# fp16 halves of the normalised input: made in natural layout and turned by DMA transposes

## What is computed

```python
xn = layernorm(x)                                   # (2, 1024, 512)
q, k, v = xn @ Wq.T, xn @ Wk.T, xn @ Wv.T           # 16 heads of 32
attn = softmax(causal(q @ k.T / sqrt(32)))
s = (attn @ v) @ Wo.T
hidden = silu(xn @ W1.T) * (xn @ W3.T)              # (2, 1024, 2048)
g = silu(fwht(hidden) @ W2.T)                       # Walsh-Hadamard transform
out = x + s * g
```

## Time and profile before

| | |
|---|---|
| median of 2 runs | 951.73 us (951.0 to 952.46) |
| span of the profiled execution | 949.5 us |
| PE busy | 936.6 us (99%) |
| VectorE busy | 728.2 us (77%) |
| ScalarE busy | 613.9 us (65%) |
| GpSimd busy | 340.2 us (36%) |

### The profile page before, as it was taken

One profiled execution on the slowest core, in us unless ns is written; L12 is line 12 of the kernel. 1 busy time (PEld: TensorE's weight loads), 2 busy tenths in 40 slices (PEclk: granted clock), 3 DMA queues, 4 the chain that ended last, 5 costly groups with the idle time before them and its releaser, 6 DMA issues. The chain is left out here.

```text
span 949.5 us, 18956 instructions
## 1 busy us (share of the span) xinstructions
PE 936.6 (99%) x6498; PEld 635.5 (67%) x6498; DVE 728.2 (77%) x1407; ACT 613.9 (65%) x1316; POOL 340.2 (36%) x590
## 2 busy tenths in 40 slices
PE   8999999999999999999999999999999999999997
PEld 7765556666665656888888656656666666588886
DVE  7987998998998988746565579899899898833343
ACT  4445889888888886723344358887888878832221
POOL 1896663665665442000000114344453443500000
PEclk9999999999999999999999999999999999999999
DMA  9797346543342405961136623323223231190111
GB/s 290 255 271 217 89 114 157 144 115 101 101 123 69 124 23 179 355 215 59 48 115 229 200 56 81 88 62 102 64 79 91 57 95 42 46 370 29 45 45 45
DMA packets 57920, 118.48 MB, mean 125 GB/s; under 512 B 5600, under 2 KB 22624, under 8 KB 57312
## 3 DMA queue, kind: packets, MB, share of 16 engines
q1 hardware_dynamic: 57824, 117.27, 40.8%
HBM read 83.43 MB, written 33.55 MB: 123 GB/s over the span
## 5 line engine op out<-in xcount | busy, mean ns | idle before, releaser
L1178 DVE TENSOR_TENSOR p_lo<-stages,p_hi 128x512 f16<-128x512 f32 (+2 forms) x288 | 199.7, 703 | 24.9 <-ACT p_hi L844 24.0
L1516 PE MATMUL f<-x_hi,w_lo 128*128 128x512 f16 x512 | 195.6, 382 | 0.0
L1516 PE MATMUL f<-x_lo,w_hi 128*128 128x512 f16 x512 | 194.8, 380 | 0.0
L1516 PE MATMUL f<-x_hi,w_hi 128*128 128x512 f16 x512 | 194.5, 380 | 0.0
L834 ACT ACTIVATE stages<-s 128x512 f32<-128x512 f32 (+2 forms) x288 | 150.5, 523 | 57.9 <-PE s L1476 55.3
L844 ACT ACTIVATE p_hi<-stages 128x512 f16<-128x512 f32 (+2 forms) x288 | 160.3, 557 | 27.5 <-POOL stages L670 18.6
L1476 PE MATMUL s<-qk_st 98*128 98x512 f32 (+2 forms) x384 | 130.0, 417 | 0.4 <-DMA qk_st<-m_lo 0.3
L670 POOL TENSOR_SCALAR_AFFINE_SELECT stages<-stages 128x128 f32<-128x128 f32 x192 | 61.5, 326 | 164.9 <-ACT stages L834 164.5
L678 POOL TENSOR_TENSOR w_lo<-w,w_hi 128x256 f16<-128x256 f32 x128 | 95.5, 775 | 55.2 <-ACT w_hi L876 52.8
L1165 DVE CUSTOM_DVE_ANT_0 m<-m,causal 128x1024 f32<-128x1024 f32 (+1 forms) x98 | 104.5, 1066 | 2.7 <-PE m L1457 1.3
L1245 DVE TENSOR_TENSOR h_lo<-hidden,h_hi 128x1024 fp32r<-128x1024 f32 x32 | 39.2, 1224 | 84.6 <-ACT h_hi L927 84.6
(11 more groups left out here) (208 smaller groups left out, 1989.1 us busy)
## 6 DMA issues: line engine op xcount, KB each, us to landing
qk_st<-qk_parts SPq DMA_DIRECT2D x96, 256.0 KB, 4.4
w<-w1w SPq DMA_DIRECT2D x32, 512.0 KB, 3.6
qk_parts<-qk_hi SPq DMA_DIRECT2D x32, 256.0 KB, 3.5
qk_parts<-qk_lo SPq DMA_DIRECT2D x32, 256.0 KB, 4.2
scan<-w1w SPq DMA_DIRECT2D x12, 512.0 KB, 5.3
wht_in<-w SPq DMA_DIRECT2D x4, 1024.0 KB, 10.6
w_butterflied<-wht_in SPq DMA_DIRECT2D x4, 1024.0 KB, 5.7
w_transformed<-g_hi SPq DMA_DIRECT2D x8, 512.0 KB, 3.7
```

The lines of the kernel that those rows point to most:

```text
L1178: dve.tensor_tensor(p_lo[s][:], expd[q % NE][:, 0:end - need], p_hi[s][:], ALU.subtract).then_inc(p_lo_done, 1)
L1516: mm = pe.matmul(F[m][:, 0, :], w, v, start=k == 0, stop=k == GMM - 1)
```

## The change

The fp16 parts are no longer made from the PSUM transposes. ACT makes `xn_hi` (128 rows x 512 columns, fp16) from the tile of `xb`, VectorE `xn_lo` from `xb` and `xn_hi`, at the same places of the order as `x16` before. Then SP issues two DMA transposes, `xn_hi` to `x16_hi` and `xn_lo` to `x16_lo`. There are two slots for each of `xn_hi` and `xn_lo`: the nth tile's ACT operation waits until both DMAs of tile n - 2 have landed. The V groups wait for the landing in place of `x16_lo_done`. SP waits for all of them after group 11, before the stack loads, since the slots share memory with a stack. PE's transposes into a bank wait for `xt_lo` of four tiles earlier only; so do the two matmul steps that use bank M.

```diff
+            with ExitStack() as q:
+                xn_hi = [sb(f"xn_hi{i}", [P, D], F16, q) for i in range(2)]
+                xn_lo = [sb(f"xn_lo{i}", [P, D], F16, q) for i in range(2)]
             qk_st.insert(0, sb("qk_st0", [P, 2, S], F32R, r))
...
+        def x16_slot(b, t):
+
+            return (x16_no(b, t) - 1) % 2
+
+        def x16_landed(no):
+
+            return (no + 1) // 2 * 32
...
+                    for t in X16_AFTER.get(g, ()):
+                        transpose_x16(b, t)
                     if g == FIRST_STACK:
 
+                        for i in range(2):
+                            sp.wait_ge(x16_in[i], x16_landed((b + 1) * NT - 1 + i))
...
+            def transpose_x16(b, t):
+                slot = x16_slot(b, t)
+                sp.wait_ge(xn_lo_done, x16_no(b, t))
+                for dst, src in ((x16_hi, xn_hi), (x16_lo, xn_lo)):
+                    sp.dma_start_transpose(dst[:, :, t * P:(t + 1) * P], src[slot][:]).then_inc(x16_in[slot], 16)
...
             def x16(b, t):
-                act.wait_ge(xt_lo_done, b * NT + t + 1)
-                act.activation(x16_hi[:, :, t * P:(t + 1) * P], xt_bank(t).rearrange("p (k c) -> p k c", k=KT),
-                               ACT.Copy, scale=X_TOP).then_inc(x16_hi_done, 1)
+                no, slot = x16_no(b, t), x16_slot(b, t)
+                act.wait_ge(xn_done, b * NT + t + 1)
+                if b > 0 and no == b * NT + 1:
+                    for i in range(2):
+                        act.wait_ge(y_stored[i], 1 + b * (NT // 2) * 16)
+                if no > 2:
+                    act.wait_ge(x16_in[slot], x16_landed(no - 2))
+                act.activation(xn_hi[slot][:], xb[:, t, :], ACT.Copy, scale=X_TOP).then_inc(xn_hi_done, 1)
...
             def x16(b, t):
-                dve.wait_ge(x16_hi_done, x16_no(b, t))
-                at = (slice(None), slice(None), slice(t * P, (t + 1) * P))
-                dve.scalar_tensor_tensor(x16_lo[at], xt_bank(t).rearrange("p (k c) -> p k c", k=KT), X_TOP,
-                                         x16_hi[at], ALU.mult, ALU.subtract).then_inc(x16_lo_done, 1)
+                slot = x16_slot(b, t)
+                dve.wait_ge(xn_hi_done, x16_no(b, t))
+                dve.scalar_tensor_tensor(xn_lo[slot][:], xb[:, t, :], X_TOP, xn_hi[slot][:], ALU.mult, ALU.subtract
+                                         ).then_inc(xn_lo_done, 1)
...
             def transpose_xn(b, t):
                 pe.wait_ge(xn_done, b * NT + t + 1)
                 if t >= 4:
-                    pe.wait_ge(x16_lo_done, x16_no(b, t - 4))
+                    pe.wait_ge(xt_lo_done, b * NT + t - 3)
...
                         pe.wait_ge(wv_lo_done, (b + 1) * KT)
-                        pe.wait_ge(x16_lo_done, x16_no(b, t))
+                        pe.wait_ge(x16_in[x16_slot(b, t)], x16_landed(x16_no(b, t)))
```

## The result

The changed kernel takes 965.06 us (median of 2 runs, 964.79 to 965.33) against 951.73: a ratio of 1.0133, interval 1.0099 to 1.0167. That is 13.3 us slower. The time lies inside the forecast range, 8 us under the forecast itself, on the faster side of the likeliest case (970 to 990) and inside that of rival 1. A loss over 2% had been given 0.57, one within 2%, which came, 0.42.

A forecast was written before the change was run, and what follows sets the result against it. PE bounds the kernel, busy 936.6 of 949.5 us. To 951.7 the prediction added 19.2 for batch 0 (VectorE's waits and contention) and 2.5 for batch 1: 973.4, forecast 973 us, range 958 to 1012 for 8 in 10.

The forecast's parts named there:

- the likeliest case: Transposing DMAs on SP's queue with an issue of 1.2 to 2.2 us: 970 to 990 us, chance 0.41.
- rival 1: At ACT's slot wait: DMAs as quick as plain ones, loss too small to tell; 956 to 970 us, chance 0.38.
- the first chain: Batch 0: ACT waits for slots, VectorE for ACT; group 8 starts 9.5 us later, the V groups 19.2.
- pair 6: Batch 0: the sixth tile's two DMAs land at 63.2 and cost VectorE 0.7 us of waiting.
- the wait before the transposes of `v_scale`: PE in the changed profile, batch 0: idle some 5 us there.
- The freed bank: PSUM bank free earlier: PE's 0.5 us wait goes, but only brings PE sooner to group 8.
- L: Time from VectorE's release of a DMA pair to its landing: 2 x 1.5 + 4.5 = 7.5 us.
- the contention: VectorE's low part slowed beside POOL, about 1.48 us each: +7.0 us in batch 0, 0 in batch 1.
- the forecast case: The likeliest case: transposing issues of 1.2 to 2.2 us on SP's queue, 970 to 990 us, chance 0.41.
- the stack loads are hidden by 2 us or more: SP at group 11, ahead of the first `qk_st` loads: waiting for landings costs nothing, with 2 us or more to spare.
- rival 2: DMAs hold SP's queue 3 us each or more: 1004 us at 3.0 and 4.5, 1029 at 4 and 6; chance 0.17.
- +2.5: Batch 1, group 8: `xt_lo` 7 ends at 514.8 instead of 511.3, less 1.0 us of slack.

The follow-up runs named there:

- four_slots: The changed kernel with four slots instead of two for xn_hi and xn_lo: 965.2 us, ratio 1.0134.
- unwaited: The kernel before, with sixteen transposing DMAs per batch added on SP's queue into memory that nothing reads: 966.04 us, ratio 1.0139.
- after: The changed kernel itself, against the kernel before: 965.06 us, ratio 1.0133.
- four_slots_scan: The changed kernel with four slots and the scan load issued after group 6 instead of 10: 962.85 us, ratio 1.0117.

## Why the prediction was right, and where it was wrong

**Right: the sign, and the first chain.** ACT waits for slots at the tiles named (third, fourth, and the one after group 8) and VectorE idles there; PE is late at group 8 and the V groups. The waits forecast as 4.9, 2.4 and 6.1 us were 2.31, 0.99 and 3.87. The fourth, 0.7 for pair 6, wasn't there; 0.41 stands in its stretch, before a `qk_lo`, because ACT's copy came late. PE waited 4.71 and 2.77 us, where near 10, 5 and 5 had been forecast; the wait before the transposes of `v_scale` did not come. The freed bank brought no gain that can be seen.

**Mis-sized: L.** It was put at 7.5 us, 2 x 1.5 of issue and 4.5 to the landing. Measured for the first pair: released at 26.43 + 0.69 = 27.12, landed at 32.46, so L = 5.3, of which 2.6 are the issues. The term that was off is the landing behind the last issue, 2.7 instead of 4.5; it had been taken from stores of 256 KB in a crowded stretch. By the Trainium skill ("Advanced Engine Details and Errata", X-Bar Transpose (TRN2)) transposing DMAs are as fast as regular ones: for the landing the runs agree (medians from the start of the issue, 2.9 and 3.2 us), for the hold on the queue they don't (1.26 and 0.63 us).

**Mis-sized: the contention.** The low part took 8.68 us for eight in batch 0. By the prediction's own way that is 8.68 - 8 x 0.60 = +3.9, not +7.0. The first ran before POOL began; of the seven beside POOL's steps two took 0.7 all the same and five 1.1 to 1.8, and what sets which is not shown. `wv_lo`, the nearest row, took 1490 ns again.

With both sizes put right the same chain gives VectorE +6.0 of idle time (2.31 + 0.99 + 3.87 + 0.41 and 0.68 more before a `qk_lo`, less the 2.24 of before), +3.9, and about -1 of other steps (`wv_abs` and `v_scale` shorter by 1.6, the scaling of Wv longer by 0.5): +8.9, against +19.2 forecast; group 8 +3.5 instead of +9.5. It is rival 1's case (L under 6.9), though the issues were not as quick as that rival wanted; it held 0.38 of the chance where the forecast case held 0.41.

**Wrong: that the stack loads are hidden by 2 us or more.** The step looked only at the batch in which everything else is late. The whole content of SP's queue moves with its sixteen issues, and four_slots and unwaited show that this alone costs what the change costs. The prediction carried it only as part of L and in rival 2, at 3 us each.

**Right size by luck, wrong place: batch 1.** +2.5 was forecast at group 8 through `xt_lo` 7. Group 8 lost nothing (+10.65 behind the kernel before, as the first scores of batch 0 were +10.2). The 2.5 us come at the first use of a stack, and SP's queue in order of time says why:

```profile
537.95 1.23 SPq L520 DMA_TRANSPOSE x_hi<-xn_hi  x1
539.22 1.26 SPq L520 DMA_TRANSPOSE x_lo<-xn_lo  x1
540.53 0.58 SPq L488 DMA_DIRECT2D qk_parts<-qk_hi  x1
...
542.16 0.46 SPq L488 DMA_DIRECT2D qk_parts<-qk_lo  x1
542.92 2.87 SPq L399 DMA_DIRECT2D qk_st<-qk_parts  x6
```

and in the kernel before:

```profile
525.00 0.43 SPq L476 DMA_DIRECT2D qk_parts<-qk_lo  x1
525.66 2.70 SPq L387 DMA_DIRECT2D qk_st<-qk_parts  x6
```

The issues stand back to back and the loads leave 17.3 us later, while PE is 10.7 late. Before, the same queue paused about 1.9 us between two pairs of stores.

**Not foreseen: the clock** behind PE's waits; it cost at least 0.7 us of the 1.3 that the V groups of batch 0 lost. Together the parts are 8.9 + 1.3 + 0.5 + 2.5 = 13.2 us: the time came into the range because the one big term, the chain, had been put too high, while a term of its own, the queue behind the issues, was missing.

**What stays open.** The single items on SP's queue (stores, scan load, stack loads) were not each freed alone in batch 0, so the 9.6 us of the transposing kind are not split among them and the clock. Why the clock fell after some waits and not after others is open too. No form of the change beat the kernel before: the best without any DMA is 954.9, since PE had 1% of idle time to give and VectorE's low part costs more beside POOL.

## What to carry to other kernels

Price a new DMA first by the time that it holds its issuing queue, and list what stands behind it on that queue with the moment at which each is needed; then by its landing. Where two delays end at the same stage they don't add: remove one and the other shows, so an edit that removes one wait and leaves the time unchanged has not shown that wait to be free. Look at the granted clock behind each new wait of PE: where PE sets the pace, it can cost as much again as the wait. In this kernel VectorE's low part read from PSUM took no longer beside a busy POOL; the same step with both sources in SBUF did.

## What the runs showed of the hardware

- A transposing DMA of 128x512 fp16 held SP's queue for 1.26 us, an ordinary one of the same rows 0.61 to 0.66, a transposing one of 128x1024 1.57. One, issued right behind the store of a 1024 KB slab, held it 3.90.
- Issued by ACT, it held ACT itself: 1.3 and 1.8 us for the first pair, and no activation in between.
- The packets rose by 75328 - 57920 = 17408, 544 for each of the 32 DMAs; with ordinary ones by 16896, 528 each, and with the sixteen merged ones by the same 16896, 1056 each.
- After 4.71 us without a matmul the granted clock was 0.51 in the next stretch of 5 us and 0.80 in the one after; after 2.77 us it was 0.66. With ordinary DMAs and four slots it fell to 0.50 after a wait of 2.09 us. It stayed at 1.00 after 2.30 us (`after`, batch 1) and after 3.3 us (`four_slots_scan`, batch 0). At 0.50 a matmul of 512 columns followed another after 0.43 us instead of 0.22.
- VectorE's subtraction with a 32-bit and a 16-bit source, both in SBUF, took 0.68 us alone and 0.7 to 1.8 beside POOL's additions; the one that reads PSUM stayed at 0.68.
